# Edge sums in four column groups of TensorE, eight steps in one run, one placing product for each eight

## What is computed

```
m   = x[src] * rel[edge_type]
m   = concat([m[:half] @ W_in, m[half:] @ W_out])
deg = segment_sum(ones, dst);  norm = 1 / max(deg, 1)
agg = segment_sum(m * norm[dst], dst)
h   = x + res * tanh(agg + x @ W_loop + b)
```

## Time and profile before

| what | value |
|---|---|
| three runs | 1937.36, 1939.32 (median), 1941.78 us |
| span of the profiled execution | 1937.8 us, 1.5 us under the median of the runs |
| instructions | 28847 |
| TensorE matmul, share of the span | 94% |
| GpSimd (POOL) | 68% |
| VectorE | 64% |
| ScalarE | 33% |

### The profile page before, as it was taken

The page is one execution under the profiler, slowest core; times in us unless marked ns, Lnnn a source line. Parts: engine busy times, 40 slices in busy tenths (PEclk is TensorE's granted clock), DMA queues, the critical chain, the costliest instruction groups (busy, mean ns, idle before and its releaser), DMA issues.

```text
span 1937.8 us, 28847 instructions
## 1 busy us (share of the span) xinstructions
PE 1821.0 (94%) x9176; PEld 1505.8 (78%) x9176; DVE 1248.8 (64%) x3345; ACT 632.8 (33%) x1552; POOL 1322.3 (68%) x1301
## 2 busy tenths in 40 slices
PE   2899899999899999999999789998899999999999
PEld 1567787887588888768888667876788888888998
DVE  6786465674855576486466645868765666654766
ACT  4452233343323333332333222332121211223443
POOL 6777777777777777777777757777777777770000
PEclk9999999999999999999999989999999999999999
DMA  9568666667776666687677856667766766661000
GB/s 274 177 198 258 203 191 206 186 202 222 243 209 199 204 194 198 208 249 214 193 218 220 274 190 229 190 200 224 229 182 215 209 199 200 190 181 17 15 28 28
DMA packets 194575, 371.44 MB, mean 192 GB/s; under 512 B 37993, under 2 KB 126095, under 8 KB 194430
## 3 DMA queue, kind: packets, MB, share of 16 engines
q0 software_dynamic: 77632, 223.91, 40.6%
q1 hardware_dynamic: 92228, 126.68, 19.9%
q10 hardware_dynamic: 24570, 19.04, 3.4%
HBM read 305.39 MB, written 64.95 MB: 191 GB/s over the span
## 4 chain that ended last, share of the span: by engine, by line
PE 80%; DVE 8%; issue 3%; DMA 3%; POOL 2%; SPq 2%; ACT 2%; DVEq 0%; ACTq 0%
PE ps_down L2765 16%; PE ps_hid L2753 16%; PE ps_seg L2629 15%; PE ps_kv L2662 5%; PE ps_x L2717 4%; PE ps_x L546 3%; PE ps_hid L3229 2%; PE ps_kv L3082 2%; POOL xg L959 2%; PE ps_hid L2682 1%; DVE xg L1055 1%; PE ps_kv L2795 1%; PE ps_down L2795 1%; DMA h_rows<-qT_all 1%; PE ps_hid L3220 1%
## 5 line engine op out<-in xcount | busy, mean ns | idle before, releaser
L959 POOL DMA_INDIRECT xg<-h_rows,idx_tab x416 | 437.2, 1051 | 143.3 <-issue 114.0
L906 POOL DMA_INDIRECT rg<-relation_rows,idx_tab x416 | 426.7, 1026 | 133.5 <-issue 126.1
L959 POOL DMA_INDIRECT xg<-xn_rows,idx_tab x416 | 423.4, 1018 | 131.9 <-issue 120.3
L2629 PE MATMUL ps_seg<-xg,hot 128*125 128x257 f32 x1664 | 414.8, 382 | 19.7 <-DVE xg L1055 19.5
L2753 PE MATMUL ps_hid<-hT,wff 128*128 128x250 f32 (+1 forms) x1920 | 368.3, 341 | 1.0 <-issue 0.8
L2629 PEld LDWEIGHTS ps_seg<-xg,hot 128*125 128x125 f32 x1664 | 305.3, 188 | 75.0 <-DVE xg L1055 19.2
L2765 PE MATMUL ps_down<-wff,gT 128*125 128x256 f32 x1600 | 363.6, 381 | 0.0
L2753 PEld LDWEIGHTS ps_hid<-hT,wff 128*128 128x128 f32 x1920 | 312.8, 189 | 37.9 <-issue 7.9
L1055 DVE TENSOR_TENSOR xg<-xg,rg 128x512 f32<-128x512 f32 x416 | 285.8, 687 | 70.8 <-DMA rg<-relation_rows,idx_tab 52.0
L2765 PEld LDWEIGHTS ps_down<-wff,gT 128*125 128x125 f32 x1600 | 295.2, 188 | 41.3
L2204 ACT ACTIVATE gT<-ps_hid,b1p 128x250 f32<-128x250 f32 (+1 forms) x480 | 177.8, 433 | 291.6 <-PE ps_hid L2753 291.5
(11 more groups left out here) (378 smaller groups left out, 2385.5 us busy)
## 6 DMA issues: line engine op xcount, KB each, us to landing
second_relation_rows<-rg SPq DMA_DIRECT2D x104, 512.0 KB, 4.1
rg<-second_relation_rows SPq DMA_DIRECT2D x104, 512.0 KB, 4.1
wff<-L_mix_W ACTq DMA_DIRECT2D x8, 1024.0 KB
rg<-relation_rows,idx_tab POOLq DMA_INDIRECT x416, 3.5
xg<-xn_rows,idx_tab POOLq DMA_INDIRECT x416, 3.2
xg<-h_rows,idx_tab POOLq DMA_INDIRECT x416, 3.6
h_rows<-qT_all SPq DMA_DIRECT2D x25, 112.0 KB
qrow<-h_rows ACTq DMA_DIRECT2D x25, 112.0 KB
```

The lines of the kernel that those rows point to most:

```text
L906: pool.indirect_dma_start(rg[:, k, :], None, rel_d, bass.IndirectOffsetOnAxis(ap=idx_tab[:, step, 1:2], axis=0))\
L959: pool.indirect_dma_start(xg[:, k, 0:D], None, rows, bass.IndirectOffsetOnAxis(ap=idx_tab[:, step, 0:1], axis=0))\
L2629: ins = pe.matmul(ps_seg[u // UW % 2][0:T, 0:AW], hot[:, s % HOTS, :], xg[:, s % RING, :], start=s % WIN == 0, stop=s % WIN == WIN - 1)
```

## The change

Edges are sorted by destination, so two neighbouring steps (250 edges) reach over few nodes. The new kernel gives each such *pair* of steps its own first node, and one-hots of 32 columns from there on. The eight steps of a window go to four column groups of TensorE (32 columns each): step s to group s % 4, by a permutation of the steps in `idx_tab` and `key_tab` (`spread_steps`, `by_groups`) that gives steps of one pair the same group. All eight run at the window's last unit, and one signal of four counts follows. VectorE copies the 128 x 257 sums from PSUM to `step_sums` and makes a one-hot `placed` (128 x 125) that says where in the window each of the 4 x 32 rows belongs; TensorE multiplies the two into the same bank (`place_sums`), and both masked additions follow.

```
-HOTS = 8
+HOTS = 16
+SPAN = 32
+COLS = P // SPAN
+QUAD = COLS
...
+                def copy_sums(self, w):
+                    dve.tensor_scalar(placed[:, :], iota_t[:, :], place_tab[:, w:w + 1], None, ALU.is_equal)
+                    dve.wait_ge(s_seg, self.g * UNITS + (UW * (w + 1) + RU))
+                    dve.tensor_copy(step_sums[:, :], ps_seg[w % 2][:, 0:AW]).then_inc(s_cps, 1)
...
                 def add(self, w, m):
                     if m == 0:
-                        dve.wait_ge(s_seg, self.g * UNITS + (UW * (w + 1) + RU))
+                        dve.wait_ge(s_plc, self.g * WINS + w + 1)
...
-                    hs = at % HOTS
-                    dve.wait_ge(s_seg, g * UNITS + (k + 1 + RU - HOTS // UNIT))
-                    dve.tensor_tensor(hot[:, hs:hs + UNIT, :], iota_t[:, :].unsqueeze(1).broadcast_to([EP, UNIT, T]),
-                                      key_tab[:, at:at + UNIT].unsqueeze(2).broadcast_to([EP, UNIT, T]), ALU.is_equal)
+                    if at % QUAD == 0:
+                        hs = at % HOTS
+                        dve.wait_ge(s_seg, g * UNITS + (k + QUAD // UNIT + RU - HOTS // UNIT))
+                        dve.tensor_tensor(hot[:, hs:hs + QUAD, :], iota_t[:, 0:SPAN].unsqueeze(1).broadcast_to([EP, QUAD, SPAN]),
+                                          key_tab[:, at:at + QUAD].unsqueeze(2).broadcast_to([EP, QUAD, SPAN]), ALU.is_equal)
...
-                    if k % UW in (2, 3) and k > UW:
-                        self.add(k // UW - 1, k % UW - 2)
+                    if k > UW and k % UW == 1:
+                        self.copy_sums(k // UW - 1)
+                    if k > UW and k % UW == 3:
+                        for m in range(2):
+                            self.add(k // UW - 1, m)
...
                 def unit(self):                       # TensorE
                     u = self.done
+                    w = u // UW
                     self.done += 1
-                    if u % UW == 0:
-                        pe.wait_ge(s_acc, (self.g * WINS + u // UW) * 2 + 1)
+                    if u % UW == 1 and w:
+                        self.place_sums(w - 1)
+                    if self.done % UW:
+                        return
+                    steps = range(w * WIN, (w + 1) * WIN)
+                    pe.wait_ge(s_acc, (self.g * WINS + w) * 2 + 1)
                     pe.wait_ge(s_msg, self.g * UNITS + (u + 2 + RU))
-                    for s in range(u * UNIT, (u + 1) * UNIT):
-                        ins = pe.matmul(ps_seg[u // UW % 2][0:T, 0:AW], hot[:, s % HOTS, :], xg[:, s % RING, :],
-                                        start=s % WIN == 0, stop=s % WIN == WIN - 1)
-                    ins.then_inc(s_seg, 1)
+                    for s in steps:
+                        rows = slice(s % COLS * SPAN, (s % COLS + 1) * SPAN)
+                        ins = pe.matmul(ps_seg[w % 2][rows, 0:AW], hot[:, s % HOTS, :], xg[:, s % RING, :],
+                                        start=s % WIN < COLS, stop=s % WIN >= WIN - COLS, tile_position=(0, rows.start))
+                    ins.then_inc(s_seg, UW)
+
+                def place_sums(self, w):
+                    pe.wait_ge(s_cps, self.g * WINS + w + 1)
+                    pe.matmul(ps_seg[w % 2][0:T, 0:AW], placed[:, :], step_sums[:, :], start=True, stop=True).then_inc(s_plc, 1)
```

More of the change, by code:

```diff
@@ L72, in build @@
     UNITS, WINS = STEPS2 // UNIT, STEPS2 // WIN
-    assert all(n % UNIT == 0 for n in STEPS_FRONT + STEPS_JOINT + sum(STEPS_GROUP, ())) and RING % WIN == 0 and HOTS == WIN
+    assert all(n % UNIT == 0 for n in STEPS_FRONT + STEPS_JOINT + sum(STEPS_GROUP, ())) and RING % WIN == 0 and HOTS % WIN == 0
     SCH = STEPS // 2
@@ L183, in build @@
         rg2 = rg[:, :, :].rearrange("p r (h d) -> p (r h) d", h=2)
-        hot = sb("hot", [EP, HOTS, T])
+        hot = sb("hot", [EP, HOTS, SPAN])
+        step_sums = sb("step_sums", [P, AW])
+        placed = sb("placed", [P, T])
+        place_tab = sb("place_tab", [P, WINS])
         iota_t = sb("iota_t", [EP, T])
@@ L280, in build @@
         spans = scratch(SCH, 4 * EP).rearrange("p (c t) -> p c t", c=4)
-        first, tile_of, base, place, bad, due = (scratch(SCH, 4) for _ in range(6))
+        both_first = scratch(SCH, 8)
+        first, pair_first = both_first[:, 0:4], both_first[:, 4:8]
+        tile_of, base, place, pair_place, bad, due = (scratch(SCH, 4) for _ in range(6))
         reached = scratch(SCH, 4 * (NT - 1)).rearrange("p (c t) -> p c t", c=4)
@@ L285, in build @@
         tile_row = scratch(1, WINS)
-        quad_first = scratch(SCH, SCH)
+        quad_first, pair_pick = (scratch(SCH, SCH) for _ in range(2))
+        row_i, row_in_span = scratch(P, 1).bitcast(I32), scratch(P, 1)
+        in_window, of_window = scratch(SCH, WIN), scratch(SCH, SCH // WIN)
+        pick_pair = scratch(SCH, P)
+        pair_places = scratch(SCH, 4 * (SCH // WIN)).rearrange("p (c w) -> p c w", c=4)
+        over = scratch(P, WINS)
         pair_a, pair_b = (flat_r[0:PAIR_ROWS, i * PAIRS:(i + 1) * PAIRS].bitcast(I32) for i in range(2))
@@ L871, in _ @@
             pool.memset(quad_first, 0.0)
+            pool.memset(pair_pick, 0.0)
             pool.iota(part_i, [[0, 1]], base=0, channel_multiplier=1)
@@ L881, in _ @@
                                pattern=[[-WIN, SCH // WIN], [0, WIN]], channel_multiplier=1)
+            pool.affine_select(out=pair_pick, in_=pair_pick, compare_op=ALU.not_equal, fill=1.0, base=0,
+                               pattern=[[-2, SCH // 2], [0, 2]], channel_multiplier=1)
             pool.memset(xg[:, :, D:AW], 1.0)
@@ L3015, in iteration @@
                 aside(8)
+                if (lay, gi) == (L - 1, NG - 1):
+                    edges.flush()
                 if f:
@@ L3118, in dense @@
                         turn_sums(t + 1)
+                    if t and among(t - 1) == AMONG > among(t - 2):
+                        edges.flush()
                     product(t, half_rows(0, t, split_tile), loop_rows(0))
@@ L3244, in _ @@
             pe.wait_ge(s_pdve, PD_ROWS)
-            pe.matmul(ps_hid[0][0:SCH, 0:4], quad_first, step_rows_f[:, 1, :, 0], start=True, stop=True).then_inc(s_ppe, 1)
+            pe.matmul(ps_hid[0][0:SCH, 0:4], quad_first, step_rows_f[:, 1, :, 0], start=True, stop=True)
+            pe.matmul(ps_hid[0][0:SCH, 4:8], pair_pick, step_rows_f[:, 1, :, 0], start=True, stop=True).then_inc(s_ppe, 1)
             pe.wait_ge(s_wqkv, 5 * 16)
@@ L3250, in _ @@
             pe.wait_ge(s_pdve, PD_FALLS)
+            pe.matmul(ps_hid[0][:, 64:64 + WINS], pick_pair, pair_places.rearrange("p c w -> p (c w)"), start=True, stop=True)
             pe.matmul(ps_hid[1][:, 0:1], ones[0:PAIR_ROWS, :], nfall, start=True, stop=False)
```

54 lines of the change are left out of this document (39 added, 15 removed).

## The result

The changed kernel took 2008.35 us, median of 4 runs (2007.7 to 2012.02), the kernel before 1938.34 us, median of 4 (1937.23 to 1941.78). The ratio is 1.0365, with a 95% interval of 1.0344 to 1.0386: 70.0 us slower, where 1917 us was forecast. The direction was wrong, and the time lies outside the range.

The account below looks back on a forecast made before the run. POOL was taken as full from 21.6 to 1738 us, with TensorE full at the same time: two engines tied. The terms -(31.1 - 20) - 15 - 4 + 4 + 4 = -22 us gave 1917 us from 1939.3; range 1900 to 1972.

Parts of the forecast that it names:

- Release of the slots: POOL's waits for edge sums, with eight slots freed at once: 20 of 31.1 us kept, bounds 0 and 31 and as much again.
- VectorE bounds nothing: VectorE: net 44 us less of 1249 us work; it sets no pace and only stretches gathers.
- the gathers eat the gain: Rival at POOL: side by side works, but waits stay at 31 us or grow; 1938 us, chance 0.08.
- POOL waiting above 40 us: Sign at POOL's waits that would show the prediction wrong; the forecast itself had waits for edge sums near 20 us.
- Added waits: Waits between VectorE's copy and TensorE's placing: only the two flushes cost, 2 us each; loss 4 us, bounds 2 and 6.
- the column groups: TensorE's edge products: a window's run takes 1.2 us in place of 3.47; with placing, TensorE is relieved of 191 us.
- half side by side: Rival at TensorE's edge products: a step costs one record, a run 2.28 us; 1943 us (1930 to 1955), chance 0.30.
- not side by side: Rival at TensorE's edge products: no overlap, 4.23 us a window in place of 3.47; 2020 us (1985 to 2040), chance 0.14.
- end lag: End of the second layer, last gather to last edge products: 24.9 us down to 10; gain 15 us, bounds 8 to 16.
- gathers' means: POOL's gathers, stretched by VectorE's work beside them: less such work gains 4 us, bounds 0 and 20.
- TensorE waits for messages above 100 us: Sign at TensorE: its waits for VectorE's message, 19.5 us in front of line 2629 before, would exceed 100 us.
- The clock's 4 us: TensorE idles in front of windows, so some stretches run at the lower clock: loss 4 us, bounds 0 and 15.

Follow-up runs that it names:

- e3: Kernel before, products as they were, but POOL is told that slots are free only by eight, with one-hots on their own signal: 1997.39 us, +58.5 against before.
- e4: Changed kernel without copy of the sums, placed one-hot and placing product; additions wait for the edge products: 1975.61 us, +36.7 against the kernel before.
- e5: Changed kernel with slots released by four and without copy, placed one-hot and placing product: 1924.17 us, -13.0 against the kernel before.
- e10: Changed kernel releasing by four, same work, but TensorE's product waits for no copy and the additions not for the placing: 1937.60 us, +0.6 against the kernel before.
- e8: Kernel before with POOL told of free slots by four instead of two, nothing else: 1946.93 us, +9.8 against before.

## Why the prediction was wrong

**The step that failed: "Release of the slots".** The prediction put POOL's waits at 20 us, "bounds 0, and 31 and as much again". Measured: 112.4 us, past the upper bound of 62, and e3 prices that step by itself at 58.5 us of time, where 11 us of gain were entered. The working of the room was right: 10.8 us in the second layer, 10.6 by the rows. What was set against it was wrong. The lag of 8.9 us was taken at the hand-over, where POOL was the bound. The second layer's own rows showed another lag: 24.9 us at its end, and POOL was already held up 25.0 us in it with 14 steps of room. Read for each of its 52 windows, the lag in the kernel before is 8.8 to 24.3 us with a median of 14.6, over the room in 43. The 8.9 us, which are 7.9 from the gather's end, lie below all of them. In the example above the lag is 24.7 us: a window waits for what stands ahead of it in two fixed orders, VectorE's and TensorE's, and what goes beyond the room is POOL's wait. So "VectorE bounds nothing" is true of its busy share and not of its order. In the first layer two gathers a step make the room 21 us, and the stretch grew by 11 us only; in the second by 64.

The rival "the gathers eat the gain" named this place and was given 0.08 and a price of only 10 us over the waits of before. Its argument against, "a second window of eight is always in work", is the error itself: with 16 slots and release by eight, a second window is all that there is. The prediction's own sign of being wrong, POOL waiting above 40 us, came true.

**Also mis-sized: "Added waits", +4.** Only the two flushes were priced, on the ground that "VectorE is a unit ahead". The chain costs 33 us (e4), and with release by four 31 (e5), 17 of it two of its waits (e10). TensorE waited for the copy 44.6 us in 23 places, VectorE for the run 31.2 in 17 and for the placing 42.9 in 25. A unit ahead is two gathers, 2.7 us of the eight that take 10.6; in the example VectorE's next message alone is 8.7 us later than the one before it (1323.46 against 1314.72). The work, too, was put down as a saving, as VectorE's total fell by 23 us (44 forecast); e10 puts the work and the wait for the run at a cost of 14 us. That work added where an engine is late does not cancel with work saved where it waits is a reading of this, and was not tested. A wait that the prediction left at nothing is in none of these sums: the two additions now follow one another, and the second waits for the first, 29.5 us in 104 places (0.6 in two before). It is in e4, e5 and e10 too, so it sits in what the column groups gave, and its price in time is not known.

**Right: the column groups.** A run of sixteen records takes 1.07 us in 96 of 104 runs (1.2 forecast), and the whole relief is worth 23 us (e5 against e8), where the forecast had gains of 30 less 4 for the clock. That POOL's pace limits the gain was right as well: 283 us less of edge products (419.8 us busy in e8, 136.4 in e5) gave 23. The rivals "half side by side" and "not side by side" fall. The Trainium skill (TensorE: Matmul & The Clock Gate, part 3 "Packing small matmuls") states that matmuls start and end strictly in program order; read as the first rival read it, a run would take 2.28 us, and the trace gives 1.07. The measurement decides against that reading. The order itself is not shown here, as no view names a record's column group; the starts come in fours, some 7 ns apart, with 0.22 us from one four to the next.

**Nearly right or small.** The end lag fell by 8 us (15 forecast, 8 the lower bound): it is 17 us, not 10. The gathers' means fell by 38 ns in the second layer alone and rose by 8 in the first for node rows: 13 us in all with the relation rows' 2 ns (4 forecast, 20 the bound); that VectorE's work is what stretches them was not tested. "TensorE waits for messages above 100 us" was wrong: 23.5 us, since the runs stand behind dense products, and most of the idle time lies in front of those and of the placing. The clock's 4 us (bounds 0 and 15) were not measured: no run changes the clock alone. What it costs is part of the terms below.

**The sum.** Column groups -23 (e5 less e8), release by eight +58.5 (e3), the chain +33 (after less e4): +69 us, where +70.0 was measured. e3 and e8 were made of the old products and e4 and e5 of the new, so the sum is a test of whether the terms are independent: e4 should be 58.5 - 23 = +36, and is +36.7.

**Open.** No version with the placing in it beat the kernel before; e5 at 1924 us, which lacks it, is what a free placing would give with release by four in this order of the work. More slots of `xg`, which attack the failed step directly, were not tried. Why two extra slots cost 10 us and four more 49 was read from the lags, and not tested by changing the stages' order.

## What to carry to other kernels

A ring's room is its slots less those released at once, and a coarser release is paid where that room is shorter than the time that a finished load waits for its consumer's place in a fixed order. Don't take that lag from a quiet stage: here one stage's shortest lag was 8.8 us, its median 14.6 and its longest 24.3. Count, for each stage, how many of its own lags are above the new room. Making the release coarser can be tried by itself in the old kernel, by its signals alone, before the new products are written. A step that sends a result from TensorE to VectorE, back and again to VectorE has three hand-overs to wait for: here copy, one-hot and placing, some 1.4 us a window in their instructions, cost 31 to 33 us.

## What the runs showed of the hardware

The four column groups work side by side for f32 to the full: in 96 of the 104 runs in the trace four records start some 7 ns apart, the next four 0.22 us after the first four, and so on for the sixteen, where records of 125 columns start 0.217 us apart one by one. That is four times for four groups; the last start comes 0.694 us after the first, and the last record's 0.38 us make up the 1.07. The weight load is shorter too (duration ns min/median/max, of the changed kernel, then of the kernel before):

```profile
L2685 PEld LDWEIGHTS ps_seg<-xg,hot x1664: 105/110/178, 69.0 to 1827.4; 128*32 128x32 f32 x185
```

```profile
L2629 PEld LDWEIGHTS ps_seg<-xg,hot x1664: 183/188/336, 55.4 to 1761.8; 128*125 128x125 f32 x185
```

What entering and leaving the mode costs was put at 0.33 us a run. By the starts in the two traces it is about 0.19. From a record of line 2830 to the run's first start are 0.309 us where the kernel before has 0.216, and from the run's last start to the next product 0.310 where it has 0.216. The second surprise is the clock: the records of all other products cover 1497 us of the span before and 1579 after (overlaps counted once), that is 82 us or 5.5% more, at a mean granted clock of 0.936 in place of 0.990. So over a third of the 227 us that the edge work gave up (414.8 - 117.6 - 70.6) came back as longer records of the same dense products.
